# Attention of a graph network on one Trainium2 core: probabilities by source, on transposed counts, summed for five destination blocks at once

## What is computed

```python
def _gat_layer(x, src, dst, W, a_src, a_dst, bias, concat):
    h = (x @ W).reshape(N, H, C)
    al_s = jnp.einsum('nhc,hc->nh', h, a_src)
    al_d = jnp.einsum('nhc,hc->nh', h, a_dst)
    e = jax.nn.leaky_relu(al_s[src] + al_d[dst], 0.2)
    m = jax.ops.segment_max(e, dst, num_segments=N)
    ex = jnp.exp(e - m[dst])
    denom = jax.ops.segment_sum(ex, dst, num_segments=N)
    alpha = ex / (denom[dst] + 1e-16)
    out = jax.ops.segment_sum(h[src] * alpha[:, :, None], dst, num_segments=N)
    return (out.reshape(N, H * C) if concat else out.mean(axis=1)) + bias

h = jax.nn.elu(_gat_layer(x, src, dst, W1, att_src1, att_dst1, b1, concat=True))
out = _layernorm(x + _gat_layer(h, src, dst, W2, att_src2, att_dst2, b2, concat=False))
```

## Time and profile before

| | us |
|---|---|
| median of 3 runs | 1036.93 (1036.09 to 1037.1) |
| the profiled execution | 1031.99 |
| its span in the trace | 1030.2 |
| mean granted PE clock | 0.963 of full |

### The profile page before, as it was taken

The page is one execution under the profiler, slowest core; times in us unless marked ns, Lnnn a source line. Parts: engine busy times, 40 slices in busy tenths (PEclk is TensorE's granted clock), DMA queues, the critical chain, the costliest instruction groups (busy, mean ns, idle before and its releaser), DMA issues.

```text
span 1030.2 us, 13905 instructions
## 1 busy us (share of the span) xinstructions
PE 913.7 (89%) x4740; PEld 786.4 (76%) x4740; DVE 619.3 (60%) x1305; ACT 401.3 (39%) x574; POOL 210.1 (20%) x113
## 2 busy tenths in 40 slices
PE   0676788979999999999999999979999998479996
PEld 0454566668787788878887788869999998479995
DVE  9666568379987456863578645443221222988874
ACT  6454531256651366514663155542111112622220
POOL 1002000225530145202442023410000000343432
PEclk9987999989999999999999999989999999689998
DMA  6009975040115410263003431252111100101122
GB/s 155 1 7 191 150 227 171 7 128 27 32 32 191 179 31 29 66 219 126 30 30 102 138 103 37 93 191 111 58 63 40 74 6 1 44 21 57 59 64 69
DMA packets 38710, 86.65 MB, mean 84 GB/s; under 512 B 17251, under 2 KB 17411, under 8 KB 37032
## 3 DMA queue, kind: packets, MB, share of 16 engines
q1 hardware_dynamic: 38663, 86.04, 29.1%
HBM read 64.27 MB, written 21.76 MB: 84 GB/s over the span
## 4 chain that ended last, share of the span: by engine, by line
issue 38%; PE 27%; DVE 10%; ACT 8%; POOL 8%; SPq 4%; DMA 4%; DVEq 0%; POOLq 0%; ACTq 0%
PE ps L1243 7%; PE ps L1245 7%; PE ps L1244 7%; POOL prow L419 5%; SPq L501 4%; DVE junk_w L1032 2%; POOL W1lo L629 2%; PE ps L1353 2%; DMA hidden_scratch<-ebuf 2%; DMA xT_scratch<-xa 1%; PE ps L1274 1%; ACT prow L414 1%; DVE nbr L437 1%; DVE prow L456 1%; ACT oh_lo L701 1%
## 5 line engine op out<-in xcount | busy, mean ns | idle before, releaser
L419 POOL TENSOR_TENSOR prow<-prow,arow 125x1250 f32<-125x1250 f32 x50 | 139.3, 2789 | 633.4 <-ACT prow L414 633.4
L1243 PE MATMUL ps<-hhi,PThi 125*125 125x512 f32 x400 | 162.2, 405 | 1.0 <-DVE hlo L1019 1.0
L1244 PE MATMUL ps<-hlo,PThi 125*125 125x512 f32 x400 | 158.5, 396 | 0.0
L1245 PE MATMUL ps<-hhi,PTlo 125*125 125x512 f32 x400 | 158.1, 395 | 0.0
L425 ACT ACTIVATE prow<-prow,expb 125x1250 f32<-125x1250 f32 x50 | 67.0, 1340 | 172.7 <-POOL prow L419 151.5
L1243 PE MATMUL ps<-W2p,hT 128*125 128x384 f32 x320 | 110.6, 346 | 6.7 <-DVE W2p L1129 5.6
L1245 PE MATMUL ps<-W2p,hT 128*125 128x384 f32 x320 | 108.7, 340 | 0.0
L1244 PE MATMUL ps<-W2p,hT 128*125 128x384 f32 x320 | 108.5, 339 | 0.0
L1088 DVE TENSOR_TENSOR hT<-ps,hT 128x500 fp32r<-128x500 f32 x40 | 25.3, 674 | 128.4 <-ACT hT L797 124.0
L476 PE MATMUL ps<-ident,prow 125*125 125x125 f32 x500 | 68.1, 286 | 28.4 <-DVE prow L456 12.2
L476 PEld LDWEIGHTS ps<-ident,prow 125*125 125x125 f32 x500 | 65.0, 199 | 35.0 <-issue 30.6
(11 more groups left out here) (157 smaller groups left out, 1818.2 us busy)
## 6 DMA issues: line engine op xcount, KB each, us to landing
xr<-xT_scratch SPq DMA_DIRECT2D x30, 750.0 KB, 4.4
hidden_scratch<-ebuf SPq DMA_DIRECT2D x40, 250.0 KB
hblk<-hidden_scratch SPq DMA_DIRECT2D x10, 1000.0 KB
xT_scratch<-xa SPq DMA_DIRECT2D x20, 375.0 KB, 13.2
w1raw<-in_L_gnn_W SPq DMA_DIRECT2D x4, 1536.0 KB, 7.7
w1raw<-in_L_gnn_W SPq DMA_DIRECT2D x12, 512.0 KB, 3.6
w2late<-in_L_gnn_W SPq DMA_DIRECT2D x10, 384.0 KB, 8.0
xres<-in_x SPq DMA_DIRECT2D x10, 375.0 KB
```

The costliest lines, as they stand in the source:

```text
L419: pool.tensor_tensor(buf[:, s, :], buf[:, s, :], row, ALU.add).then_inc(e_done, 1)
L1243: pe.matmul(dst, ahi, bhi, start=start, stop=False)
L1244: pe.matmul(dst, ahi, blo, start=False, stop=False)
L1245: return pe.matmul(dst, alo, bhi, start=False, stop=stop)
```

## The change

**Sources in the partition.** Counts stay as the windows make them, `C` with the source in the partition. A probability row is now made for one block of sources and half of the destinations (625 columns, a *chunk*). ACT's relu and exp take the source's score as bias, the destination's score comes as a row spread over partitions (`drow`), and POOL adds a row `grow`, which holds the destination's score less its maximum. The chunk can be a stationary operand as it is, so the 500 transposes of rows go. ACT copies the high part and DVE subtracts for the low part, both from the buffer in SBUF where they read PSUM before.

**Order.** A head has 20 chunks: ten source blocks for destination blocks 0 to 4, then ten for 5 to 9. All five destination blocks of a half accumulate at once in five banks and share the rest of them: each 512-column product is cut in two at `SPLIT`, and its small part lies beside the large part of its neighbour. `h` gets two columns of ones (`hx`), whose sum is the denominator. In the second half of a head a make of h for the next head follows each chunk, in banks 6 and 7, and overwrites the block of h just used. A ring of three holds chunks.

**Maxima.** They need the destination in the partition, so masks (0 or -1e30, bf16) are made once from transposed counts, stored in DRAM by ACT's queue and loaded again for each head. The ten maxima of a head must be done before its first chunk; those of the next head stand at places listed in `plan_max`. The shift goes through PE's spread in head 0, through DRAM for the others.

**Layer 2.** 20 chunks again, in a ring of eleven; first half in three pieces a block (`CUT`, `PLACE`, `ORDER2`), all eight banks; second half one destination block after another, in two pieces of 384 and 386 columns. All probabilities are made before the first eviction. Two W2 blocks more are split during the last head. Loops of the heads are written out.

```diff
+GT = NB // 2
+PR = 3
+SPLIT = (260, 258, 256, 254, 252)
+PR2 = 11
-        def pe_transpose(pe, g, s, buf):
-            for bank, (lo, hi) in enumerate(TCH):
-                for b in range(lo, hi):
-                    t = pe.transpose(PS[0:B, 2 + bank, (b - lo) * B:(b - lo + 1) * B], buf[:, s, b * B:(b + 1) * B], ident[0:B, 0:B])
+        def act_relu(act, c):
+            h, g, b = chunk_of(c)
+            if c >= PR:
+                act.wait_ge(pt_lo, c - PR + 1)
...
+        def dve_counts(dve, c):
+            h, g, b = chunk_of(c)
+            dve.wait_ge(p_done, c + 1)
+            dve.scalar_tensor_tensor(pslot(c), pslot(c), 1.0, C[:, b, g * GN:(g + 1) * GN], ALU.min, ALU.mult).then_inc(pc_done, 1)
+        def act_hi(act, c):
+            act.wait_ge(pc_done, c + 1)
+            if PR <= c < CHUNKS:
+                act.wait_ge(ag, ag_at(c - PR))
...
+            act.activation(hi_slot(c), pslot(c), ACT.Copy).then_inc(pt_hi, 1)
+        def dve_lo(dve, c):
+            dve.wait_ge(pt_hi, c + 1)
+            dve.tensor_tensor(lo_slot(c), pslot(c), hi_slot(c).bitcast(F32), ALU.subtract).then_inc(pt_lo, 1)
...
         @block.vector
+            def evict(q, t):
+                h, n = q // 2, GT * q + t
+                dve.wait_ge(ag, ag_block(q, t))
+                dve.tensor_scalar(deps[:, n:n + 1], acc_big(t)[:, in_bank(t) - 1:in_bank(t)], 1e-16, None, ALU.add).then_inc(d_eps, 1)
...
+            plan_max = {(0, 0): (0,), (0, 1): (1,), (0, 8): (2,), (0, 9): (3,), (1, 0): (4, 5), (1, 1): (6, 7), (1, 3): (8, 9)}
+            for c in range(CHUNKS):
+                h, g, b = chunk_of(c)
+                if b == 2 and c >= NB:
+                    for t in range(GT):
+                        evict(c // NB - 1, t)
+                dve_lo(dve, c)
+                if c + 1 < CHUNKS:
+                    dve_counts(dve, c + 1)
+                if g == 0 and b < 3 and h > 0:
+                    split_h(NB * h + NB - 3 + b)
+                if 3 <= b < 3 + GT and c >= NB:
+                    elu(GT * (c // NB - 1) + b - 3)
+                if h + 1 < H:
+                    for m in plan_max.get((g, b), ()):
+                        maxima(h + 1, m)
...
         @block.tensor
+            def chunk(c):
+                pe.wait_ge(pt_lo, c + 1)
...
+                for t in range(-1, GT):
+                    if t + 1 < GT:
+                        if b == 0 and q > 0:
+                            pe.wait_ge(v_done, GT * (q - 1) + t + 2)
+                        piece(t + 1, True)
+                    if t >= 0:
+                        last = piece(t, False)
+            for c in range(CHUNKS):
+                chunk(c)
+                if g == 1 and h + 1 < H:
+                    make(h + 1, b)
```

More of the change, by code:

```diff
@@ L275, in gat_kernel @@
         ld_b2 = sem("ld_b2")
-        ld_xres = [sem(f"ld_xres{i}") for i in range(2)]
+        ld_xres = [sem(f"ld_xres{i}") for i in range(3)]
         out_stored = sem("out_stored")
@@ new lines, in _ @@
+            sp.wait_ge(nb_stored, 16 * NB)
+            for b in range(MR):
+                load_nb(0, b)
+            sp.wait_ge(rows_sb, 3)
+            sp.dma_start(rows_d[:, :], rows[:]).then_inc(rows_stored, 16)
+            sp.wait_ge(rows_stored, 16)
+            load_drow(0, 0)
+            for b in range(MR, NB):
+                load_nb(0, b)
+            sp.wait_ge(rows_ps, 3)
+            sp.wait_ge(mk_done, NB)
+            load_drow(0, 1)
+            sp.dma_start(b1row[:], spread_row(b1)).then_inc(ld_b1, 16)
@@ L680, in _ @@
+            for n in range(3):
+                add_bias(n)
+            for c in range(CHUNKS + 4, CHUNKS + 2 * NB):
+                pool_add(pool, c)
+            for n in range(3, 8):
+                add_bias(n)
+            for n in range(NB):
+                pow_var(n)
+                if GT <= n and n + 3 < NB:
+                    add_bias(n + 3)
         @block.scalar
@@ new lines, in h2_out @@
+            def h2_out(b):
+                act.wait_ge(h2_ps, 2 * b + 2)
+                act.activation(h2f[:, b, :].rearrange("p (a n) -> p a n", a=2), h2_banks(b % 2), ACT.Copy).then_inc(h2_sb, 1)
+            split_hT(0)
+            act.wait_ge(ag, ag_at(CHUNKS - 1))
+            split_w2(8)
+            split_w2(9)
+            elu(H * NB - GT)
+            elu(H * NB - GT + 1)
+            split_w2(10)
+            split_w2(11)
+            for n in range(2, GT):
+                elu(H * NB - GT + n)
@@ new lines, in lo_w2 @@
+            def lo_w2(c):
+                dve.wait_ge(w2_hi, c + 1)
+                dve.tensor_tensor(W2p[:, c, 1, :], w2_raw(c), W2p[:, c, 0, :].bitcast(F32), ALU.subtract).then_inc(w2_lo, 1)
+            split_hT(0)
+            for t in range(GT):
+                evict(NG - 1, t)
+            lo_w2(8)
+            lo_w2(9)
+            elu(H * NB - GT)
+            elu(H * NB - GT + 1)
+            lo_w2(10)
+            lo_w2(11)
+            for n in range(2, GT):
+                elu(H * NB - GT + n)
@@ new lines, in make @@
+            def make(h, b):
+                u = NB * (h - 1) + b
+                if b == 0:
+                    pe.wait_ge(w1_lo, KD * (h + 1))
+                pe.wait_ge(h_lo, NB * h + b - 1)
+                pe.wait_ge(ld_xr[u % XR], 16 * (u // XR + 1))
+                for k in range(KD):
+                    t = products(make_bank(b),
+                                 ((xr[:, u % XR, 0, k * B:(k + 1) * B], xr[:, u % XR, 1, k * B:(k + 1) * B]),
+                                  (W1hi[:, k, :], W1lo[:, k, :])), k == 0, k == KD - 1)
+                t.then_inc(mk_done, 1)
@@ L1397, in mm_half @@
+            for c in range(CHUNKS):
+                h, g, b = chunk_of(c)
+                chunk(c)
+                if g == 1 and h + 1 < H:
+                    make(h + 1, b)
+                if c == CHUNKS - 2:
+                    transpose_h(0)
+            def mm_half(n):
+                b, half = n // 2, n % 2
+                pe.wait_ge(ht_lo, n + 1)
                 for k in range(KH):
                     c = half * KH + k
-                    if isinstance(b, int) and b == 0:
+                    if b == 0:
@@ new lines, in _ @@
+            for c in range(NB):
+                pe.wait_ge(pt_lo, CHUNKS + c + 1)
+                pe.wait_ge(h2_lo, c + 1)
+                for u, order in enumerate(ORDER2):
+                    for t, i, first in order:
+                        last = piece2(c, t, i, first)
+                    if c == NB - 1 or u == GT - 1:
+                        last.then_inc(ag2, 1)
+            for t in range(GT):
+                pe.wait_ge(y_b, (2, 3, GT, GT, GT + 1)[t])
+                for b in range(NB):
+                    if t == 0:
+                        pe.wait_ge(pt_lo, CHUNKS + NB + b + 1)
+                    for i in range(2):
+                        last = piece2(NB + b, t, i, True)
+                last.then_inc(ag2, 1)
```

1230 lines of the change are left out of this document (643 added, 587 removed).

## The result

The changed kernel takes 1107.96 us (median, 1104.15 to 1111.41), the kernel before took 1037.01 beside it: ratio 1.0685, 95% interval 1.0642 to 1.0728. Forecast were 1060 us and 1003 to 1090. Slower was right; two thirds of the loss were not foreseen.

The account below looks back on a forecast made before the run. Heads were taken as a TensorE stream, to be stalled by a VectorE-GpSimd lock. -52.9 + 78.4 + 4.5 - 5.5 - 1.8 = +22.7 on 1036.9 gave 1060 us, range 1003 to 1090.

Parts of the forecast that it names:

- Before the heads: Ahead of the score rows: counts lose a transposed copy, gain a mask written to DRAM; 0 us (-3 to +2).
- Start of the heads: Before the first attention matmul: all ten maxima come first, then the chain to the first chunk; +4.5 us (0 to +8).
- fourth rival: Masks come late: 50 loads on SyncE's queue, 1 us on 20 maxima ahead of evictions; 1080 us, chance 0.06.
- Stalls of the heads: Four heads: TensorE waits at the turn to the other five destinations; 72.4 plus 6 for slow clock, +78.4 us.
- The step that names the cause: Heads: GpSimd operations and VectorE operations with both inputs in SBUF exclude each other; locked time 2.82 us a chunk.
- four gaps of 8 to 13 us: Sign of being right: one TensorE gap in each head, ended by VectorE's reciprocal-and-evict lines.
- Bare work: Heads' TensorE stream: 40 sets of ten transposes go, halves cost nothing extra; 406.6 instead of 459.5, -52.9 us.
- third rival: Weight loads do not fit beside halved matmuls: at 0.14 us between starts, 1095 us; chance 0.06.
- W2: Product with W2: eight blocks split beforehand instead of six, waits and slow clock 9.4 become 3.9; -5.5 us.
- Layer 2: Second layer's attention: later start and a middle wait against transposes removed; -1.8 us, ends -18 and +10.
- middle gap: Middle of layer 2: TensorE waits 14 us because VectorE makes all twenty chunks before it evicts.
- first and second rival: First: VectorE stays ahead, GpSimd taking little lock, 984 us (0.14). Second: half the stalls, lock partly shared, 1013 us (0.12).

Follow-up runs that it names:

- Experiment 2: Changed kernel with only the last of ten masks stored and every load reading that one; ratio 1.0478 to the kernel before, span 1082.9.
- experiment 1: Changed kernel with masks staged in two SBUF buffers by turns instead of one; ratio 1.0587 to the kernel before, span 1094.5.
- experiment 3: Changed kernel with two staging buffers and early loads of attention vectors and the first three of W1; ratio 1.0511 to the kernel before, span 1082.1.
- experiment 4: Changed kernel with a ring of five loaded masks instead of three; ratio 1.0605 to the kernel before, span 1094.8.
- experiments 5: Changed kernel with five loaded masks and eight of the next head's ten maxima moved behind the evictions; ratio 1.0298 to the kernel before, span 1065.4.
- Experiment 6: Changed kernel with GpSimd adding one column instead of 625 in each of 100 chunks; ratio 1.0274 to the kernel before, span 1058.7.
- experiment 8: Changed kernel with layer 2's first two evictions before the low part of chunk 16 of 20; ratio 1.0632 to the kernel before, span 1099.5.
- runs 1 to 10: The first ten follow-up runs, all edits of the changed kernel, singly or combined; ratios to the kernel before from 1.0632 to 0.9951.

## Why the prediction was wrong

**Before the heads, forecast 0 (-3 to +2), measured +24.7: the step that failed.** It priced the store of a mask at nothing because "folding of W1 stays behind SyncE's stores of xT, both untouched". Both were touched: 3.1 MB joined DMA engines without room, and one staging buffer made ScalarE wait for the stores, 28 us in all. Experiment 2 puts 22 us on the stores, experiment 1 17 on the buffer up to the first block of h. The row of the DMA engines from 90 to 140 us in the kernel before, shown under experiment 3, was there to be read. This term alone took the time out of the range: 1108 less 24.7 is 1083.

**Start of the heads, +4.5 (0 to +8), measured +16.9.** 6.7 us are masks that land late, 4.9 of them shown by experiment 4. This is the cause of the fourth rival (at 0.06), which had put 1 us on 20 maxima ahead of evictions; its sign, VectorE waiting for a DMA ahead of maxima, is there. It acts ahead of head 0 and, with 2.0 and 2.7 us, in the turns of heads 0 and 1. Another 3.2 are the spreading, 1.1 by a wrong estimate and 2.1 by the slow clock after 17 us without work. What remains is 1.4 before the maxima and about 1 behind.

**Stalls of the heads, +78.4, measured 69: right in place, near in size partly by luck.** Chunk by chunk (starts of every thirtieth half), beyond 3.57 or 7.77 us each, heads 0 to 3 lose 23.3, 17.6, 18.1 and 10.2 us, forecast 22.1, 18.6, 18.6 and 13.1; the slow clock, 6 us of the forecast on top, is inside the measured ones. The step that names the cause holds: experiments 5 and 6 show that the order makes stalls, and that countings, subtractions and elus are held up by the adds (the countings take 1143 against 803 ns). The Trainium skill (SBUF — State Buffer, SBUF: two separate sides) calls it an exclusive lock for a whole instruction, and the trace agrees: the maximum at 434.97 ends at 437.73, 1.3 us behind the end of the add beside it (434.46 to 436.41), nearly its whole length alone (1.46).

The shares were wrong. For adds that cost the lock nothing the forecast kept 19.5 of its 78.4, so it put 59 on the lock. Experiment 6, close to that case, leaves 45: the adds are worth 24, or some 30 (an estimate) without the 5.7 us by which the waits for masks grew. What is left there beyond 19.5 lies mainly in waits for masks, which had no term (10.5 us in the turns of heads 0 and 1), and in late first chunks: that of head 0 takes 10.7 us instead of 3.57. And of the four gaps of 8 to 13 us that were to show it, three came; head 3's is 4.7.

**Bare work, -52.9, off by +5:** 0.06 us a chunk (3.57 for 3.51). This and the first wait of the W2 product (2.4 us, counted with the heads) offset most of the 9 us above. The third rival, loads that do not fit, is out: 0.119 us apart, not 0.13 or more.

**W2, -5.5, measured +2.1.** The sum was off too: the parts that it names, 1.3 and 1.7, make 3.0, not 3.9. Behind that first wait one of 5.0 us is left, and TensorE is busy 191.1 us instead of 188.3. The cause stays open; in runs 1 to 10, whose edits leave it alone, the stretch takes 194 to 200.5 us.

**Layer 2, -1.8, measured +5.0.** Its first matmul came at X+27.9 instead of X+22.3: the maxima again wait for masks and run 2.2 to 2.9 us apart instead of 1.5 from the sixth on. The middle gap was right, and experiment 8 shows its cause.

The first and second rival (VectorE ahead, half of the stalls) are out as forecasts of the time; that the lock takes less than the prediction gave it is nonetheless so. The range failed at one place: the stretch ahead of the heads was bounded by a few us, without an end for a store that must wait.

## What to carry to other kernels

A transfer added to a stretch costs nothing only if the DMA engines have room there and nobody waits for its buffer: look at their busy share and at what is queued behind the wait, not at the bytes. Where an in-order engine makes ahead and evicts, put the eviction at the step where the accumulation ends and the next head's work behind it; that was worth 29 to 32 us, with not one instruction less. When a sum comes out near, test its parts: here the heads were right within 1 us with the lock's share off by half. And after removing a gap, follow the time to the end: twice here it came back as a wait in another queue.
